# Joined bias loads, spaced weight loads and a later table switch in the prologue; both value blocks of a unit side by side

## The chip, the cores and the metric

The kernel runs on one core of one Trainium2 chip. The metric is device time of one execution in microseconds (us); lower is better. TensorE is called PE, VectorE DVE, ScalarE ACT, GpSimd POOL and SyncE SP, as the profile does.

## The reference, cut to what matters

The input `x` is (128, 32, 512): batch, channel, position. A 32x32 matrix per batch item, picked from 16, mixes the channels; the result goes through an attention over the 32 channels with 32 heads and low-rank queries and keys; then come a masked long convolution over the 512 positions (by FFT in the reference, by Toeplitz matmuls in the kernel) and a dequantised linear layer, with residual sums.

```python
W = weights[condition]                        # (128, 32, 32)
h = einsum('bct,bcd->bdt', x, W)              # tokens are the 32 channels
q_c = h @ Wq_c.T + bq_c                       # 192 wide
q   = (q_c @ Wq_up.T + bq_up)                 # 32 heads of 128 + 64 (rope)
kv  = h @ Wkv_c.T + bkv_c                     # 64 nope + 64 rope
kvu = kv[..., :64] @ Wkv_up.T + bkv_up        # 32 heads: k 128, v 128
k   = concat(k_nope, broadcast(kv_rope))
a   = softmax(q @ k.T / sqrt(192))
o   = a @ v                                   # per head
x   = x + sum_over_heads(o @ Wo.T) + bo
y   = causal_conv(masked x, s4_kernel) + D * masked x     # masked again
x   = x + (y @ dequantised(qweight).T + bias)
```

## The kernel before, in words

The kernel is written with an explicit order for each engine: a function per engine that issues instructions one behind another and waits on semaphores. There is no scheduler; the order on each engine is the order in its function, and a waiting instruction holds all behind it.

The attention is worked off in 16 units (`NU`): 8 groups of 16 batch items (`k`), and of each two halves of 16 heads (unit `u`, group `u // 2`, half `u % 2`). The key up-projection is folded into the query one: for each head a 192x64 matrix M is made once from two weights (`products`, `weights_high`, `weights_low`; 8 weight groups `g` of 4 heads), so the scores are formed against the 64-wide latent. All large matmuls have operands split into a high and a low part, three matmuls for one.

What a unit does, in PE's order (`u` from 2 to 14):
- `fold(u, j0, j1)`: for the heads j0 to j1, latent queries times M into PSUM; two heads at a time in banks 0 and 1 (`BT`) or 2 and 3 (`BS`). Each head is evicted to `qt` by ACT, heads 13 and 15 by DVE (`late_head`). Heads j, j+1 may only start when the two heads four before them are evicted.
- `values(u - 1, m_)`: the probabilities of the unit before times the latent, in two value blocks `m_` of 8 heads, 32 matmuls each (the trace has two records for each, 64 in all), into four PSUM banks. ACT copies each bank to `z_high`, DVE makes `z_low` from bank and copy. Before, `values(u - 1, 0)` stands between heads 0 to 13 and heads 14, 15 of the fold, `values(u - 1, 1)` behind the fold.
- `scores(u, n)`, n = 0 to 3: DVE turns each into `sc` (`take_scores`), takes off the maximum (`below_max`), ACT exponentiates (`soft`), DVE sums, divides and turns (`normalised`) into `pT`.
- `output(u - 1, n)`: z times the value weight, in four parts. In odd units `project` (x times the compressing weights, four token blocks n, per block 8 matmuls with the high and 4 with the low part of x), the copies `feat` of its result on ACT (`feat_taken`) and `mix_features` stand between these parts, for the next group; in even units `turn_latent` follows.

Unit 0 has its own order: `project_first`, `products(0)`, `mix_features(0)`, `products(1)`, then four heads of fold and one `products` in turn, `scores(0, n)`, `products(6)`, `products(7)`. This and unit 1 are called the prologue here. SP issues most transfers in program order, ACT the small bias loads, POOL the gathers of the condition matrices (`gathered`), which it masks into `mix`. The last unit, the convolution and the linear layer (from 575 us on) are not touched.

## Time and profile before

| | us |
|---|---|
| median of 3 runs | 725.34 (724.9 to 725.49) |
| the profiled execution | 725.95 |
| its span in the trace | 724.0 |
| PE busy in the span | 705.0 |
| DVE busy | 597.2 |
| ACT busy | 412.6 |
| POOL busy | 215.3 |

The span is from the first to the last recorded instruction; the profiled execution's own time is 1.95 us longer. A row of the timeline gives start, duration, engine, line and operation, output and inputs, how many instructions stand in the row, and in brackets how long the engine was idle before it and what ended that. Matmuls overlap, so the distance from one start to the next tells more than a duration.

### The profile page before, as it was taken

The numbers are of one execution on the slowest core, as the hardware profiler recorded it, in microseconds if no ns is written. First come the engines' busy times: TensorE is split into PE (matmuls) and PEld (weight loads), VectorE is DVE, ScalarE is ACT, GpSimd is POOL, SyncE is SP. The second block draws the span as 40 slices with busy tenths as digits, with TensorE's granted clock in tenths as the row PEclk, the third lists the DMA queues.
The fourth block names the chain that finished last, engine by engine and source line by source line (L and its number), as shares of the span: only waits on it lengthen the run. The fifth ranks groups of instructions, "written<-read, shape, count | busy, mean of one in ns | idle before, by whom it ended". The sixth has DMA issues, their size and how long they took to land.

```text
span 724.0 us, 17041 instructions
## 1 busy us (share of the span) xinstructions
PE 705.0 (97%) x7154; PEld 567.1 (78%) x7154; DVE 597.2 (82%) x1005; ACT 412.6 (57%) x736; POOL 215.3 (30%) x242
## 2 busy tenths in 40 slices
PE   7999999999999999999999999999999899999997
PEld 6767777787978697878877786978677688888885
DVE  4889999998999678787769776887798689999975
ACT  4676565647556765746565656556664444444443
POOL 5461020020002010550020000003521267777884
PEclk9999999999999999999999999999999999999999
DMA  7900100010002000100100010002112587999942
GB/s 220 329 3 2 51 13 1 2 61 4 1 2 62 3 2 22 39 5 13 60 5 2 2 59 2 1 2 92 60 60 54 139 225 152 181 244 188 239 106 107
DMA packets 31919, 50.94 MB, mean 70 GB/s; under 512 B 6594, under 2 KB 21090, under 8 KB 30562
## 3 DMA queue, kind: packets, MB, share of 16 engines
q1 hardware_dynamic: 29858, 49.26, 25.0%
q8 instruction: 57, 0.93, 0.5%
q0 software_dynamic: 1024, 0.53, 0.4%
q14 instruction: 20, 0.16, 0.1%
q10 hardware_dynamic: 960, 0.06, 0.1%
HBM read 41.19 MB, written 8.63 MB: 69 GB/s over the span
## 4 chain that ended last, share of the span: by engine, by line
PE 76%; DVE 13%; ACT 4%; issue 4%; POOL 2%; DMA 1%; SPq 0%; DVEq 0%; ACTq 0%
PE ps L736 34%; PE ps L785 7%; PE ps L628 5%; PE ps L629 5%; PE ps L630 5%; PE ps L807 4%; PE ps L677 3%; PE ps L636 2%; PE ps L638 2%; PE ps L637 2%; DVE x_low L1663 2%; DVE x_t L1657 2%; DVE y L1701 1%; PE ps L1029 1%; PE ps L1037 1%
## 5 line engine op out<-in xcount | busy, mean ns | idle before, releaser
L1141 ACT ACTIVATE qt<-ps,m_bias 128x512 f32<-128x512 f32 x228 | 145.8, 686 | 87.5 <-PE ps L736 83.9
L736 PE MATMUL ps<-q_high,m_high 64*128 64x512 f32 x768 | 166.0, 397 | 0.2 <-issue 0.2
L736 PE MATMUL ps<-q_high,m_low 64*128 64x512 f32 x768 | 162.4, 388 | 0.2
L736 PE MATMUL ps<-q_low,m_high 64*128 64x512 f32 x768 | 114.4, 387 | 0.0
L736 PEld LDWEIGHTS ps<-q_high,m_high 64*128 64x128 f32 x768 | 89.5, 184 | 15.4 <-issue 5.9
L736 PEld LDWEIGHTS ps<-q_high,m_low 64*128 64x128 f32 x768 | 89.8, 184 | 9.8 <-issue 1.0
L1428 DVE TENSOR_TENSOR z_low<-ps,z_high 128x512 fp32r<-128x512 f32 x128 | 79.8, 681 | 18.7 <-ACT z_high L1161 18.7
L736 PEld LDWEIGHTS ps<-q_low,m_high 64*128 64x128 f32 x768 | 81.6, 184 | 9.8
L1161 ACT CAST z_high<-ps 128x512 fp32r<-128x512 f32 x128 | 66.7, 597 | 14.5 <-PE ps L807 9.9
L1146 ACT ACTIVATE sc<-sc 128x512 f32<-128x512 f32 x60 | 38.1, 634 | 41.5 <-DVE sc L1413 35.2
L494 POOL TENSOR_TENSOR o_sum<-o_part,o_part 128x512 f32<-128x512 f32 x7 | 9.1, 1307 | 173.2 <-ACT o_part L1171 173.2
L459 POOL TENSOR_TENSOR mix<-gathered,block_of 128x256 f32<-128x256 f32 x16 | 10.4, 667 | 161.4 <-PE ps L677 152.1
L785 PE MATMUL ps<-qt,kv 128*32 128x512 f32 x480 | 55.0, 595 | 2.7 <-ACT qt L1141 1.2
L617 POOL TENSOR_TENSOR y_low<-y,y_high 128x512 fp32r<-128x512 f32 x32 | 48.4, 1511 | 18.6 <-ACT y_high L1357 18.5
L628 PE MATMUL ps<-z_high,wvT_high 128*128 128x512 f32 (+1 forms) x132 | 53.6, 406 | 0.0
L1434 DVE TENSOR_SCALAR qt<-ps,m_bias 128x512 f32<-128x512 f32 x28 | 20.9, 750 | 37.7 <-PE ps L736 37.6
L629 PE MATMUL ps<-z_low,wvT_high 128*128 128x512 f32 (+1 forms) x132 | 50.9, 386 | 0.0
L630 PE MATMUL ps<-z_high,wvT_low 128*128 128x512 f32 (+1 forms) x132 | 50.7, 384 | 0.0
L1421 DVE TENSOR_TENSOR sc<-sc,row_stat 128x512 f32<-128x512 f32 x60 | 44.6, 743 | 2.1
L1413 DVE TENSOR_TENSOR sc<-sc,row_stat 128x512 f32<-128x512 f32 x60 | 42.9, 715 | 2.1
L1423 DVE STREAM_TRANSPOSE pT<-sc 128x512 f32<-128x512 f32 x60 | 42.7, 711 | 2.0
L611 POOL TENSOR_TENSOR rest<-rest,x_t 128x512 f32<-128x512 f32 x29 | 37.9, 1308 | 17.0 <-ACT rest L1344 17.0
(259 smaller groups left out, 1468.5 us busy)
## 6 DMA issues: line engine op xcount, KB each, us to landing
x_raw<-in_x_groups SPq DMA_DIRECT2D x32, 256.0 KB
x_t<-in_x_channels SPq DMA_DIRECT2D x8, 1024.0 KB, 7.8
out<-rest SPq DMA_DIRECT2D x32, 256.0 KB, 6.3
toep_high<-taps_scratch SPq DMA_DIRECT2D x32, 192.0 KB, 4.4
toep_low<-taps_scratch SPq DMA_DIRECT2D x32, 192.0 KB, 4.9
w_raw<-in_w_groups SPq DMA_DIRECT2D x8, 512.0 KB, 8.0
toep_far<-taps_scratch SPq DMA_DIRECT2D x32, 64.0 KB, 5.7
rope_raw<-in_rope_rows SPq DMA_DIRECT2D x8, 192.0 KB, 7.7
```

The lines of the kernel that those rows point to most:

```text
L617: pool.tensor_tensor(y_low[g % 2][:, :, ch, :], y[c % 2][:], f(y_high[g % 2][:, :, ch, :]), ALU.subtract).then_inc(s["yl_done"], 1)
L628: pe.matmul(out, lh, rh, start=start, stop=False)
L629: pe.matmul(out, lh, rl, start=False, stop=False)
L630: return pe.matmul(out, ll, rh, start=False, stop=stop)
L736: mm = pe.matmul(ps[:, fold_bank(u, j) + e, :], weights[rows, (GH * g + j) // 2, c, :], moving[c][rows, :], start=start, stop=stop)
L785: mm = pe.matmul(ps[32 * b:32 * b + 32, s_bank(u, n), :], kv[:, tok], qt[:, :, tok], start=True, stop=True)
L1141: act.activation(qt[:, j, :], ps[:, fold_bank(u, j) + j % 2, :], ACT.Identity, bias=m_bias[:, h:h + 1]).then_inc(s["qt_done"], 1)
L1161: act.copy(z_part(z_high, m_, b), z_made(u, m_, b)).then_inc(s["zh_done"], 1)
L1413: dve.tensor_tensor(rows(n), rows(n), wide(n), ALU.subtract).then_inc(s["sub_done"], 1)
L1421: dve.tensor_tensor(rows(n), rows(n), wide(n), ALU.mult).then_inc(s["norm_done"], 1)
L1423: dve.transpose(flat(pT[:, n]), flat(sc[:, n])).then_inc(s["turn_done"], 1)
L1428: dve.tensor_tensor(z_part(z_low, m_, b), z_made(u, m_, b), f(z_part(z_high, m_, b)), ALU.subtract).then_inc(s["zl_done"], 1)
```

## The change

In the prologue:
- The seven small bias loads that ACT issued behind its first casts become three: `bq_bv` (both head biases side by side) is issued by ACT as its second instruction; `latent_biases` (three columns) and `bq_rope` by SP behind weight group 0.
- Weight group 1 is loaded behind the wait for the gathers (it was loaded in front of it), group 2 behind the first mixed block (`q_ready`), groups 3 to 5 each behind a finished `products`, groups 6, 7 and the value weight behind `products(4)`.
- ACT's two sines of the state-space parameters, with the table loads in front of and behind them, move from behind the third `weights_high` inside the fold of unit 0 to behind the last eviction; the four casts of the value weight move into unit 1, and PE's `turned_par` stands four heads later.
- The normalising multiplication of unit 0 moves from DVE to POOL, ahead of POOL's `values_low`; DVE does the four sums and reciprocals first, then the four transposes.

In units 2 to 14:
- The fold of 16 heads is undivided; both value blocks stand behind it, next to each other.
- The second value block of a unit writes banks 0 to 3 (before: 0, 1, 4, 5), and `scores` goes to banks 4, 5, 7, 0 (before: 2, 3, 7, 0). So `scores(u, 0)` waits for the first `z_low` of the first value block, `scores(u, 1)` for the second one; `scores(u, 2)` and `scores(u, 3)` wait for the third and the fifth one, as before.
- `project` does the matmuls with the high part for all four token blocks first, then those with the low part for all four.
- ACT and DVE evict their last heads first and then take the value banks 0 to 3 in one row.

The core of the diff (renamed banks, input packing and the waits that only follow from them are cut):

```diff
@@ sync
-            for g in range(2):
-                load_weights(g)
+            load_weights(0)
+            sp.dma_start(columns[:, 0:3], d["latent_biases"]).then_inc(s["bias_in"], 16)
+            sp.dma_start(m_bias[64:P, :], d["bq_rope"]).then_inc(s["bias_in"], 16)
...
             for n in range(2):
                 sp.wait_ge(gather_in[n], 32)
-            for g in range(2, 6):
+            load_weights(1)
+            sp.wait_ge(s["q_ready"], 1)
+            load_weights(2)
+            for g in range(3, 6):
+                sp.wait_ge(s["fold_ready"], g - 1)
                 load_weights(g)
-            sp.dma_start(wvT_raw[:], d["wvT"]).then_inc(s["wv_in"], 16)
+            sp.wait_ge(s["fold_ready"], 5)
             load_weights(6)
             load_weights(7)
+            sp.dma_start(wvT_raw[:], d["wvT"]).then_inc(s["wv_in"], 16)
@@ tensor, project
-                    if n != 2:
-                        pe.wait_ge(s["s_taken"], 4 * u + (1, 2, 0, 4)[n])
+                    if u == 1 and n < 2:
+                        pe.wait_ge(s["s_taken"], 4 * u + n + 1)
+                    elif n < 3:
+                        pe.wait_ge(s["zl_done"], 8 * (u - 1) + (7, 8, 6)[n])
                     else:
-                        pe.wait_ge(s["zl_done"], 8 * (u - 1) + 6)
+                        pe.wait_ge(s["s_taken"], 4 * u + 4)
...
                         projected(k, n, tt, False)
+                for n in range(4):
                     for tt in range(TT):
@@ tensor, scores
-                if n == 2 and u >= 1:
-                    pe.wait_ge(s["zl_done"], 8 * (u - 1) + 3)
-                if n == 3 and u >= 1:
-                    pe.wait_ge(s["zl_done"], 8 * (u - 1) + 5)
+                if u == 1 and n >= 2:
+                    pe.wait_ge(s["zl_done"], 8 * (u - 1) + 2 * n - 1)
+                if u >= 2:
+                    pe.wait_ge(s["zl_done"], 8 * (u - 1) + (1, 2, 3, 5)[n])
@@ tensor, units 2 to 14
-                    fold(u, 0, 14)
+                    fold(u, 0, 16)
                     values(u - 1, 0)
-                    fold(u, 14, 16)
                     values(u - 1, 1)
@@ scalar, unit 0
-                if g == 2:
-                    act.wait_ge(s["sin_go"], 1)
-                    act.activation(sin1[:], ang[:], ACT.Sin).then_inc(s["sin_done"], 1)
...
-            for n in range(4):
-                values_high(n)
+            act.wait_ge(s["sin_go"], 1)
+            act.activation(sin1[:], ang[:], ACT.Sin).then_inc(s["sin_done"], 1)
...
             weights_high(6)
             weights_high(7)
+            values_high(0)
@@ gpsimd
+            for n in range(4):
+                pool.wait_ge(s["inv_done"], n + 1)
+                pool.tensor_tensor(flat(sc[:, n]).rearrange("p (r c) -> p r c", c=C),
+                                   flat(sc[:, n]).rearrange("p (r c) -> p r c", c=C),
+                                   row_stat[:, n, :].unsqueeze(2).broadcast_to([P, 2 * GP, C]), ALU.mult).then_inc(s["norm_done"], 1)
             for n in range(4):
                 values_low(n)
```

On PE, at the end of unit 2's fold and behind it, before (`q_high` and `q_low` rows are the fold, `pT` rows a value block of 32 matmuls, `qt` the four scores):

```order
L807 MATMUL ps<-pT,ctok 64x128 x32
L736 MATMUL ps<-q_high_71,m_high 128x512 x2
L736 MATMUL ps<-q_high_71,m_low 128x512 x2
L736 MATMUL ps<-q_high_73,m_high 128x512 x2
L736 MATMUL ps<-q_high_73,m_low 128x512 x2
L736 MATMUL ps<-q_high_72,m_high 128x512 x2
L736 MATMUL ps<-q_high_72,m_low 128x512 x2
L736 MATMUL ps<-q_low_74,m_high 128x512 x2
L736 MATMUL ps<-q_low_76,m_high 128x512 x2
L736 MATMUL ps<-q_low_75,m_high 128x512 x2
L807 MATMUL ps<-pT,ctok 64x128 x32
L785 MATMUL ps<-qt,kv 32x512 x16
```

and now:

```order
L753 MATMUL ps<-q_low_74,m_high 128x512 x2
L753 MATMUL ps<-q_low_76,m_high 128x512 x2
L753 MATMUL ps<-q_low_75,m_high 128x512 x2
L824 MATMUL ps<-pT,ctok 64x128 x64
L802 MATMUL ps<-qt,kv 32x512 x16
L641 MATMUL ps<-z_high,wvT_high 128x512
L642 MATMUL ps<-z_low,wvT_high 128x512
```

The last head pair of the fold stands in front of both value blocks, and the scores follow the second block in both orders.

On PE, in `project` of unit 1, before (`x_high` rows are matmuls with the high part of x, eight to a token block, `x_low` rows the four with the low part):

```order
L636 MATMUL ps<-wcT_high,x_low_65 128x320 x2
L636 MATMUL ps<-wcT_high,x_low_66 128x320 x2
L637 MATMUL ps<-wcT_high,x_high 128x320
L638 MATMUL ps<-wcT_low,x_high 128x320
L637 MATMUL ps<-wcT_high,x_high 128x320
L638 MATMUL ps<-wcT_low,x_high 128x320
L637 MATMUL ps<-wcT_high,x_high 128x320
L638 MATMUL ps<-wcT_low,x_high 128x320
L637 MATMUL ps<-wcT_high,x_high 128x320
L638 MATMUL ps<-wcT_low,x_high 128x320
L636 MATMUL ps<-wcT_high,x_low_65 128x320 x2
L636 MATMUL ps<-wcT_high,x_low_66 128x320 x2
```

and now, at the end of the same `project` (`z_high` is the output part behind it):

```order
L651 MATMUL ps<-wcT_low,x_high 128x320
L650 MATMUL ps<-wcT_high,x_high 128x320
L651 MATMUL ps<-wcT_low,x_high 128x320
L649 MATMUL ps<-wcT_high,x_low_65 128x320 x2
L649 MATMUL ps<-wcT_high,x_low_66 128x320 x2
L649 MATMUL ps<-wcT_high,x_low_65 128x320 x2
L649 MATMUL ps<-wcT_high,x_low_66 128x320 x2
L649 MATMUL ps<-wcT_high,x_low_65 128x320 x2
L649 MATMUL ps<-wcT_high,x_low_66 128x320 x2
L649 MATMUL ps<-wcT_high,x_low_65 128x320 x2
L649 MATMUL ps<-wcT_high,x_low_66 128x320 x2
L641 MATMUL ps<-z_high,wvT_high 128x512
```

The low matmuls of all four blocks are now the last 16 of the 48, and the four results become ready close together.

On ACT, in unit 0, before (`qt` rows are evictions of folded heads, `m_high` casts of the folding matrices, `sin` the two sines):

```order
L1141 ACTIVATE qt<-ps,m_bias 128x512 x4
L1112 CAST m_high<-rope_raw 128x6x64
L1115 CAST m_high<-ps 128x6x64
L1212 ACT_TABLE_LOAD
L1212 ACTIVATE sin_125<-ang 32x64
L1213 ACTIVATE sin_126<-ang 32x64
L1214 ACT_TABLE_LOAD
L1214 ACTIVATE warm<-ones 32x1
L1141 ACTIVATE qt<-ps,m_bias 128x512 x4
```

and now:

```order
L1157 ACTIVATE qt<-ps,m_bias 128x512 x4
L1128 CAST m_high<-rope_raw 128x6x64
L1131 CAST m_high<-ps 128x6x64
L1220 ACT_TABLE_LOAD
L1220 ACTIVATE sin_124<-ang 32x64
L1221 ACTIVATE sin_125<-ang 32x64
L1222 ACT_TABLE_LOAD
L1222 ACTIVATE warm<-ones 32x1
L1128 CAST m_high<-rope_raw 128x6x64
L1131 CAST m_high<-ps 128x6x64
L1128 CAST m_high<-rope_raw 128x6x64
```

The last four evictions of unit 0 stand in front of the table loads now, and two pairs of casts of the folding matrices behind them.

## Rows read from the trace of the kernel before

**Rows 1.** The page's first part: busy time of PE.
```profile
PE 705.0 (97%) x7154; PEld 567.1 (78%) x7154; DVE 597.2 (82%) x1005; ACT 412.6 (57%) x736; POOL 215.3 (30%) x242
```
**Rows 2.** Timeline of PE, unit 0: start us, us, engine line op tiles xcount [idle before].
```profile
15.03 0.92 PE L706 MATMUL ps<-w_raw 128*64 128x64 f32 x24 [1.62 <-DMA bq_n<-in_bq_nope]
...
16.06 2.94 PE L677 MATMUL ps<-mix,feat 128*128 128x128 f32 x24
...
24.60 0.92 PE L706 MATMUL ps<-w_raw 128*64 128x64 f32 x24
...
29.94 0.92 PE L706 MATMUL ps<-w_raw 128*64 128x64 f32 x24
...
36.60 0.92 PE L706 MATMUL ps<-w_raw 128*64 128x64 f32 x24
...
44.20 3.64 PE L785 MATMUL ps<-qt,kv 128*32 128x512 f32 x32 [1.16 <-ACT qt L1141]
```
**Rows 3.** Timelines of DVE, POOL and ACT, unit 0.
```profile
14.24 0.21 DVE L1499 COPY feat<-ps 128x64 f32<-128x64 f32 x1
...
9.06 0.95 POOL L449 DMA_INDIRECT gathered<-in_L_cond_weights,row_of  x1 [0.31 <-issue]
...
14.87 0.62 POOL L459 TENSOR_TENSOR mix<-gathered,block_of 128x256 f32<-128x256 f32 x1 [1.42 <-DMA gathered<-in_L_cond_weights,row_of]
...
41.77 2.37 ACT L1141 ACTIVATE qt<-ps,m_bias 128x512 f32<-128x512 f32 x4
```
**Rows 4.** Transfers: w_raw, issue to landing of eight; and qw, on a quiet queue.
```profile
DMA to landing us min/median/max: 7.2/8.0/8.2
...
qw<-in_ffn_words SPq DMA_DIRECT2D x1, 1024.0 KB, 5.2
```
**Rows 5.** Weight loads of PE, waits whose end no record shows, unit 0.
```profile
32.68 0.18 PEld L736 LDWEIGHTS ps<-q_high,m_low 64*128 64x128 f32 x1 [0.53 <-issue]
```
**Rows 6.** Timeline of PE, unit 1: values, scores, project, mixing.
```profile
67.13 1.59 PE L807 MATMUL ps<-pT,ctok 32*64 32x128 f32 x64
...
71.58 1.21 PE L807 MATMUL ps<-pT,ctok 32*64 32x128 f32 x64
...
74.28 1.07 PE L785 MATMUL ps<-qt,kv 128*32 128x512 f32 x8 [0.50 <-DVE z_low L1428]
...
78.13 0.30 PE L637 MATMUL ps<-wcT_high,x_high 128*128 128x320 f32 x1
...
87.69 2.84 PE L677 MATMUL ps<-mix,feat 128*128 128x128 f32 x24
```
**Rows 7.** Timeline of PE, unit 4: the two value blocks and the scores.
```profile
173.25 1.21 PE L807 MATMUL ps<-pT,ctok 32*64 32x128 f32 x64
...
176.66 1.20 PE L807 MATMUL ps<-pT,ctok 32*64 32x128 f32 x64
177.79 3.64 PE L785 MATMUL ps<-qt,kv 128*32 128x512 f32 x32
```
**Rows 8.** Timeline of DVE, unit 4.
```profile
175.11 1.29 DVE L1428 TENSOR_TENSOR z_low<-ps,z_high 128x512 fp32r<-128x512 f32 x2 [0.90 <-ACT z_high L1161]
...
177.46 3.67 DVE L1428 TENSOR_TENSOR z_low<-ps,z_high 128x512 fp32r<-128x512 f32 x6
181.04 2.50 DVE L1407 STREAM_TRANSPOSE sc<-ps 128x512 f32<-128x512 f32 x4
```
**Rows 9.** Timeline of PE, unit 5: project and mixing.
```profile
212.80 0.30 PE L637 MATMUL ps<-wcT_high,x_high 128*128 128x320 f32 x1
...
214.81 0.31 PE L637 MATMUL ps<-wcT_high,x_high 128*128 128x320 f32 x1
...
221.47 2.84 PE L677 MATMUL ps<-mix,feat 128*128 128x128 f32 x24
```
**Rows 10.** Timeline of ACT, unit 5: copies of feat, and an exponential.
```profile
215.01 0.43 ACT L1081 COPY feat<-ps 128x320 f32<-128x320 f32 x1 [2.69 <-PE ps L636]
...
217.19 0.65 ACT L1146 ACTIVATE sc<-sc 128x512 f32<-128x512 f32 x1
```
**Rows 11.** Start of unit 5: ACT's first evictions, and PE's third head pair.
```profile
189.69 1.27 ACT L1141 ACTIVATE qt<-ps,m_bias 128x512 f32<-128x512 f32 x2
...
191.40 0.52 PE L736 MATMUL ps<-q_high,m_high 64*128 64x512 f32 x2
```

More of the change, by code:

```diff
@@ L194, in build @@
     wvT_raw = t("wvT_raw", [P, NPAIR, P], at=wvT_at + 8 * KB)
-    bq_n = t("bq_n", [P, NH], at=zh_at)
-    bv_n = t("bv_n", [P, NH], at=zh_at + 128)
+    bq_bv = t("bq_bv", [P, 2 * NH], at=zh_at)
+    bq_n, bv_n = bq_bv[:, 0:NH], bq_bv[:, NH:2 * NH]
     cond_rows = t("cond_rows", [P, B // 4], I32, at=zh_at + 256)
@@ L293, in build @@
     BT, BS, BZ, BO, BX = 0, 2, 4, 6, 7
-    ZBANK = ((BZ, BZ + 1, BX, BO), (BT, BT + 1, BZ, BZ + 1))
+    FIRST_ZBANK = ((BZ, BZ + 1, BX, BO), (BT, BT + 1, BZ, BZ + 1))
+    ZBANK = ((BZ, BZ + 1, BX, BO), (BT, BT + 1, BS, BS + 1))
     LATE_ZBANK = ((BX, BZ, BZ + 1, BO), (BZ, BZ + 1, BT, BS))
@@ L297, in build @@
     FOLD_BANK = (BT, BS)
-    SBANK = (BS, BS + 1, BX, BT)
+    SECOND_SBANK = (BS, BS + 1, BX, BT)
+    SBANK = (BZ, BZ + 1, BX, BT)
     FIRST_SBANK = (BT, BX, BS, BS + 1)
@@ L919, in _ @@
                     turn_latent(0)
+                    fold(u, 8, 12)
                     turned_par()
-                    fold(u, 8, 16)
+                    fold(u, 12, 16)
                     values(0, 0)
@@ L1209, in _ @@
                 weights_high(g + 2)
[L1210 to L1216 removed]
+            act.wait_ge(s["sin_go"], 1)
+            act.activation(sin1[:], ang[:], ACT.Sin).then_inc(s["sin_done"], 1)
+            act.activation(sin2[:], ang[:], ACT.Sin, scale=0.5).then_inc(s["sin_done"], 1)
+            act.activation(warm[:], ones[:], ACT.Exp)
             weights_high(6)
             weights_high(7)
+            values_high(0)
             for n in range(2):
@@ L1226, in _ @@
             fold(1, 8, 10)
+            values_high(1)
+            fold(1, 10, 12)
+            values_high(2)
             act.wait_ge(s["par_turned"], 1)
             act.copy(parT[:].rearrange("p a h -> p (a h)"), ps[:, BO, 0:4 * C]).then_inc(s["parT_done"], 1)
-            fold(1, 10, 16)
+            fold(1, 12, 14)
+            values_high(3)
+            fold(1, 14, 16)
             for u in range(1, LAST):
@@ L1250, in _ @@
                         ffn_float(2)
-                    values(u - 1, 0, 0, 3)
                     fold(u, 14, 16)
-                    values(u - 1, 0, 3, 4)
+                    values(u - 1, 0, 0, 4)
                     if u == 8:
@@ L1506, in _ @@
             weights_low(1)
+            dve.wait_ge(w_in[0], 32)
+            dve.tensor_reduce(bv_sum[:], bv_n, AX.X, ALU.add).then_inc(s["bias_done"], 1)
             dve.wait_ge(s["ssm_in"], 80)
@@ L1537, in _ @@
             for n in range(4):
-                normalised(0, n)
+                dve.wait_ge(s["exp_done"], n + 1)
+                dve.tensor_reduce(stat(n), rows(n), AX.X, ALU.add).then_inc(s["sum_done"], 1)
+                dve.wait_ge(s["sum_done"], n + 1)
+                dve.reciprocal(stat(n), stat(n)).then_inc(s["inv_done"], 1)
+            for n in range(4):
+                dve.wait_ge(s["norm_done"], n + 1)
+                dve.transpose(flat(pT[:, n]), flat(sc[:, n])).then_inc(s["turn_done"], 1)
             for u in range(1, LAST):
@@ L1557, in _ @@
                 else:
-                    values(u - 1, 0, 0, 2)
                     late_head(u, GH - 1)
-                    values(u - 1, 0, 2, 4)
+                    values(u - 1, 0, 0, 4)
                 values(u - 1, 1, 0, 4)
```

37 lines of the change are left out of this document (14 added, 23 removed).

## The prediction, made before the changed kernel ran

> **What bounds the kernel now.** I read the busy shares first, then PE's timeline by units, then what ended PE's gaps. PE is busy for 705.0 of 724.0 us [rows 1], so time can only come from the 19 us of gaps, from matmuls that are stretched because their operands come late, and from the small loss at each change of kind of matmul. Two stretches matter. In the prologue PE waits visibly: 1.62 us for a bias load, 1.16 us for ACT's evictions [rows 2], and in unit 1 for z_low [rows 6]. In the 13 units from 2 to 14 PE runs almost without a gap: value blocks, head pair and scores follow each other at once [rows 7]. There the change can save only the loss at the changes, and it adds a dependence of the scores on z_low. So I work out both stretches as chains: who is late once the order is new.
>
> **Prologue.** (a) The first mixing starts at 16.06 because products(0) waits for bq_n until 15.03 [rows 2]. With the bias issued at the start, products(0) can begin where project_first ends, 15.03 - 1.62 = 13.41. Next late are DVE's copies of feat, which end at 14.24 + 0.21 = 14.45, and POOL's mix: the last gather is issued until 10.01 and the mask starts at 14.87 [rows 3]. That gather runs beside 704 KB of weight group 1, which now waits. If it lands 1.0 us earlier or more, the copies bound and the mixing starts at 14.55: gain 1.5 us. If it lands as before, the mask ends at 15.49 and the gain is 0.5. I take 1.45, since with group 1 gone less stands beside the gather. The weight loads: group 1 is issued behind the gathers, at about 13.4, and products(1) wants it when the mixing's 2.9 us are over, at 17.4. The eight weight loads landed 7.2 to 8.2 us after issue, in a full queue; twice the size on a quiet queue took 5.2 [rows 4]. I take 4.0, nearer the quiet one less half its bytes: no wait. The bound the other way is 13.4 + 7.2 = 20.6, a wait of 3.2 us. Later groups are asked for at 5.3 us steps and have over 5 us each.
>
> For that load the Trainium skill has a fit: DMA: Bandwidth & Descriptors, "Anatomy of one DMA", gives 2.0 us plus the bytes at 436 KB per us. By it, as an estimate, 512 KB take 3.2 us and products(1) doesn't wait either; the row of 5.2 us for 1024 KB is above its 4.4.
>
> (b) A stretch of one products and four heads takes 29.94 - 24.60 = 5.34 us, the next one 36.60 - 29.94 = 6.66 [rows 2]. The 1.3 us more are waits of PE's weight loads that no record ends, as the one of 0.53 us [rows 5], while transfers fill the engines. If they come from the crowded queue, spaced loads take them away. The last 3.4 MB are still loaded in one go, later. I take 0.9 of 1.3; bounds 0 and 1.6.
>
> The Trainium skill, Runtime: NRT & Kernel Launch, "Instruction fetch mechanics", speaks against (b): it says that a sequential program's fetch is hidden by the issue rate. By it these gaps aren't a matter of the queue and would stay, 0.9 us less gain; no row shows what they wait for.
>
> (c) scores(0, 0) waits 1.16 us for four evictions that began at 41.77, behind two table loads [rows 2, 3]. Without these, the last two evictions end 1.27 us (the duration of such a pair [rows 11]) behind the fold, of which products(5) hides 1.03: 0.24 is left, gain 0.9. The table loads now lie beside scores(0) and products(6), when ACT has only casts to do; POOL's chain on the sines starts some 3 us later and still ends before turned_par.
>
> (d) Unit 1: DVE ends its normalising late, and the scores behind the first value block start late. From 67.13 to the last score block at 74.28 are 7.15 us [rows 6]. The multiplications on POOL free DVE of four of its longest operations; then it is one value block (1.13), two score blocks (1.81), then from the second block's start to the gated score 74.28 - 71.58 = 2.70: 5.64. Gain 1.5. POOL has some 6 us for its four multiplications before the values, and values_low after them before the first output. (e) project of unit 1 to mixing took 9.56 us, waiting for x_low [rows 6]; with the low matmuls last and by (g) it takes 8.93. Gain 0.6. turned_par, apart from turn_latent, costs 0.1. Prologue: -1.45 - 0.9 - 0.9 - 1.5 - 0.6 + 0.1 = -5.3.
>
> **Units 2 to 14.** v is the start of the first value block. (f) Before, v to the scores is 177.79 - 173.25 = 4.54, with a head pair (2.04) inside and two changes of kind, each about 0.1. Undivided, the pair goes before v, and the scores could follow at v + 2.26, a saving of 0.24. But scores(u, 0) now waits for the first z_low. That starts at 175.11 - 173.25 = 1.86 behind v [rows 7, 8], and unit 1 shows the same chain from value block to gated score: 2.70 [rows 6]. ACT is free for it, because its one eviction ends 0.8 behind v. So before: 4.54; after: 2.04 + 2.70 = 4.74. Each unit loses 0.20, 13 units 2.6. The later score blocks find their z_low in time: z_low advances 0.60 a bank (3.67 for six [rows 8]) against 0.91 a score block; the fifth is ready at v + 5.1 for a score at v + 5.4. Bounds: -0.24 and +0.5 a unit.
>
> (g) Odd units 3 to 13: from project to mixing 8.67 us [rows 9], of which 0.25 is a wait for x_low (the first token block takes 2.01, the others 1.76). Without the wait: 8.42. In the new order the four results are ready at 5.3, 5.9, 6.4 and 7.0 behind the start. ACT must copy the first, do an exponential, copy the second, and so on; the last copy ends three exponentials and four copies later. A copy with its small second part takes 0.42 to the next start, an exponential 0.53 (0.65 long, overlapped) [rows 10]: the copies start at 5.47, 6.4, 7.4, 8.3, the last ends at 8.85, and the mixing starts at 8.93. Before, these lay a token block apart under the matmuls. So 8.93 against 8.67: +0.26, six units 1.6. What the low matmuls no longer wait for is more than given back.
>
> (h) Even units: DVE must make eight z_low behind the second block. It starts its turn of the scores at v + 1.86 + 8 x 0.60 = v + 6.64, which is 3.94 behind the scores' start; before it was 181.04 - 177.79 = 3.25 [rows 7, 8]. All that DVE does then, to the exponentials, is 0.69 later against PE, and ACT's first evictions of the next unit stand behind these exponentials. They end at 189.69 + 1.27 = 190.96; PE needs them for the third head pair at 191.40 [rows 11]. With 0.07 for the signal, 0.37 is in hand and 0.69 is asked: a wait of about 0.32, in units 3, 5, 7, 11 and 13 (behind unit 8 the tap products lie before the fold): 1.6. The convolution and the last unit's code are untouched; their wait for DVE may take up to 0.4 of the shift, a bound only.
>
> Sum: -5.3 + 2.6 + 1.6 + 1.6 = +0.5. The profiled execution took 725.95, 0.6 above the median: 726.45, and 725.9 on the median's level.
>
> **The rivals.** First, the forecast, no change. Second, faster: the chains (g) and (h) don't reach PE, because DVE or ACT has slack that I count as used; only (f) is paid. For it: ACT idles 2.69 us before the copies [rows 10]; against it: the copies can't start before their matmuls end. 725.34 - 5.3 + 2.6 = 722.6. Third, faster by more: the undivided fold does what it seems to, scores at v + 2.26: -0.24 x 13 = -3.1 in the place of +2.6, with (g) and (h): 720.1. Against it stands the gated score at 2.70 in unit 1; it would take a z_low that is ready 0.44 sooner than in any row.
>
> Fourth, slower: weight group 1 is late. It lands as the others did, at 20.6 instead of 17.4, products(1) stands in PE's queue before the whole fold, and everything waits 3.2 us: 729.1. For it: every weight load took at least 7.2; against it: they were queued behind one another. It decides from a landing 4.0 us behind its issue on. Fifth, slower: (a) gives only 0.5 and (b) nothing, so the prologue gives 3.4: 727.8.
>
> **How the numbers follow.** A measurement of this kernel tells 0.2%, 1.45 us, from no change. Chances: forecast 0.44, second 0.20, third 0.06, fourth 0.14, fifth 0.16. The forecast's own range is 724.2 to 727.6, since (f) to (h) repeat and 0.1 us a unit is 1.3; some of it lies beyond 726.8. Faster: 0.20 + 0.06 = 0.26. Slower: 0.14 + 0.16 and 0.04 of the forecast = 0.34. Same: 0.40. The range goes to the second case and the fourth: 722.2 to 729.2.
>
> **What the new profile would show.** (a) The first mixing at 14.6, products(1) without a DMA wait. (b) Stretches of 5.3 us between products. (c) No wait over 0.4 us before the first scores. (f) In every unit a gap of PE of 0.4 to 0.5 us before the scores, ended by z_low, and 2.70 from value block to scores. (g) 8.9 us from project to mixing, ended by a copy of feat. (h) A wait of 0.3 us at the third head pair of units 3, 5, 7, 11 and 13, ended by an eviction. The forecast is wrong if the scores follow the value blocks at once, if the mixing doesn't wait for feat, or if products(1) waits for its weights.

## The result

The changed kernel takes 726.18 us (median of 16 runs, 725.35 to 727.74) against 724.76 for the kernel before in the same comparison: ratio 1.0023, 95% interval 1.0014 to 1.0031. That is 1.7 us slower, about at the 0.2% from which a change can be told from none; 725.9 was forecast. One of the 16 runs of before took 865.19 us; the ratio goes by the fast runs alone, and that one isn't among them. The profiled execution took 726.38 us, with a span of 724.5 (before: 725.95 and 724.0).

The end hides two large movements. PE's timeline after, unit 0 and unit 1, answers to [rows 2] and [rows 6] (start us, us, engine, line, operation, tiles, count, [idle before <- what ended it]):

```profile
12.85 0.92 PE L723 MATMUL ps<-w_raw 128*64 128x64 f32 x24
...
14.02 2.94 PE L693 MATMUL ps<-mix,feat 128*128 128x128 f32 x24
16.89 0.92 PE L723 MATMUL ps<-w_raw 128*64 128x64 f32 x24
...
39.67 3.64 PE L802 MATMUL ps<-qt,kv 128*32 128x512 f32 x32 [0.32 <-ACT qt L1157]
...
62.66 1.21 PE L824 MATMUL ps<-pT,ctok 32*64 32x128 f32 x64
...
66.07 1.20 PE L824 MATMUL ps<-pT,ctok 32*64 32x128 f32 x64 [0.35 <-DVE z_low L1439]
...
68.76 1.06 PE L802 MATMUL ps<-qt,kv 128*32 128x512 f32 x8 [0.50 <-DVE z_low L1439]
...
72.63 0.30 PE L650 MATMUL ps<-wcT_high,x_high 128*128 128x320 f32 x1
...
81.57 2.94 PE L693 MATMUL ps<-mix,feat 128*128 128x128 f32 x24 [0.36 <-ACT feat L1098]
```

The lead over the kernel before grows from row to row: the first mixing is at 14.02 in the place of 16.06, the first scores at 39.67 in the place of 44.20, the mixing of unit 1 at 81.57 in the place of 87.69. That is 6.12 us ahead. From there the lead melts, in nearly equal steps but for units 8, 9 and 14. This table gives, from PE's timelines, how far the starts of the scores lie from those of before (negative is ahead):

```
scores of unit         2     3     4     5     6     8    10    12    14   first output projection
changed kernel     -5.81 -5.34 -4.77 -4.30 -3.74 -2.52 -2.05 -0.98 -0.33   +0.46
```

From an even unit to an odd one 0.46 to 0.50 is lost, from an odd one to an even one 0.56 to 0.65. The exceptions are unit 7 to 8 (0.74), unit 8 to 9 (0.18 won back) and unit 13 to 14 (0.19). The view of PE's waits (engine, line, what it waited for: us in total, times, longest) names two large new entries. Below them stand PE's timeline in unit 4 (answers to [rows 7]) and DVE's there (answers to [rows 8]):

```profile
PE ps L802 <- DVE z_low L1439: 7.4, 15, 0.5
PE ps L693 <- ACT feat L1098: 2.5, 7, 0.4
```

```profile
170.32 2.19 PE L824 MATMUL ps<-pT,ctok 32*64 32x128 f32 x128
173.02 3.64 PE L802 MATMUL ps<-qt,kv 128*32 128x512 f32 x32 [0.51 <-DVE z_low L1439]
```

```profile
172.18 4.88 DVE L1439 TENSOR_TENSOR z_low<-ps,z_high 128x512 fp32r<-128x512 f32 x8 [0.97 <-ACT z_high L1177]
176.97 2.50 DVE L1418 STREAM_TRANSPOSE sc<-ps 128x512 f32<-128x512 f32 x4
```

The scores follow the value block by 2.70 us, and DVE begins to turn them 3.95 us behind their start (3.25 before). PE's busy time fell by 3.8 us, and the time didn't: a fall in busy time here only says that its matmuls are stretched less and stand in longer gaps.

```profile
PE 701.2 (97%) x7154; PEld 560.0 (77%) x7154; DVE 590.9 (82%) x1001; ACT 408.5 (56%) x736; POOL 217.6 (30%) x246
```

### The profile page after: what moved, and what is told of

It is laid out like the page before. It is cut to its first block, busy times and chain, and to the rows that moved or that the text cites. A ratio compares the mean times of both kernels' runs of the same rounds, so it can differ in the third digit from the quotient of the medians.

```text
span 724.5 us, 17037 instructions
## 1 busy us (share of the span) xinstructions
PE 701.2 (97%) x7154; PEld 560.0 (77%) x7154; DVE 590.9 (82%) x1001; ACT 408.5 (56%) x736; POOL 217.6 (30%) x246
## 4 chain that ended last, share of the span: by engine, by line
PE 77%; DVE 10%; ACT 7%; issue 4%; POOL 2%; DVEq 0%; ACTq 0%
PE ps L753 37%; PE ps L802 7%; PE ps L641 5%; PE ps L643 5%; PE ps L642 5%; PE ps L693 3%; PE ps L824 3%; PE ps L650 3%; PE ps L651 3%; DVE x_low L1679 2%; DVE x_t L1673 2%; DVE z_low L1439 2%; ACT z_high L1177 2%; ACT sc L1162 2%; DVE y L1717 1%
## 5 line engine op out<-in xcount | busy, mean ns | idle before, releaser
L753 PE MATMUL ps<-q_high,m_high 64*128 64x512 f32 x768 | 158.4, 395 | 0.0
L753 PE MATMUL ps<-q_high,m_low 64*128 64x512 f32 x768 | 155.2, 387 | 0.0
L753 PE MATMUL ps<-q_low,m_high 64*128 64x512 f32 x768 | 110.6, 386 | 0.0
L753 PEld LDWEIGHTS ps<-q_high,m_high 64*128 64x128 f32 x768 | 79.8, 184 | 18.3 <-issue 3.1
L753 PEld LDWEIGHTS ps<-q_high,m_low 64*128 64x128 f32 x768 | 79.9, 184 | 12.1
L753 PEld LDWEIGHTS ps<-q_low,m_high 64*128 64x128 f32 x768 | 76.2, 184 | 12.9
L1177 ACT CAST z_high<-ps 128x512 fp32r<-128x512 f32 x128 | 64.8, 620 | 13.3 <-PE ps L824 8.5
L802 PEld LDWEIGHTS ps<-qt,kv 128*32 128x32 f32 x480 | 16.2, 108 | 35.8 <-issue 33.0
L1424 DVE TENSOR_TENSOR sc<-sc,row_stat 128x512 f32<-128x512 f32 x60 | 41.7, 696 | 2.1
L1432 DVE TENSOR_TENSOR sc<-sc,row_stat 128x512 f32<-128x512 f32 x56 | 40.6, 724 | 1.9
```

Of the source, the lines that this page charges most:

```text
L753: mm = pe.matmul(ps[:, fold_bank(u, j) + e, :], weights[rows, (GH * g + j) // 2, c, :], moving[c][rows, :], start=start, stop=stop)
L802: mm = pe.matmul(ps[32 * b:32 * b + 32, s_bank(u, n), :], kv[:, tok], qt[:, :, tok], start=True, stop=True)
L1177: act.copy(z_part(z_high, m_, b), z_made(u, m_, b)).then_inc(s["zh_done"], 1)
L1424: dve.tensor_tensor(rows(n), rows(n), wide(n), ALU.subtract).then_inc(s["sub_done"], 1)
L1432: dve.tensor_tensor(rows(n), rows(n), wide(n), ALU.mult).then_inc(s["norm_done"], 1)
```

## The experiments

Twelve runs were made, of ten kernels (pj_again and p_again repeat pj_copies and p_only), in three groups; the kernels of a group shared a chip and its runs of before. Below the first two rows the groups are the first four, the next four and the last four. "To mixing" is the time from the projection's start to the mixing in unit 3, the next two are between the starts of the scores of units 2, 3 and 4; "gaps" is what products(1) to products(5) of unit 0 took above 21.36 us.

```
kernel          ratio    95% interval     to mixing  2 to 3  3 to 4   gaps
before          1                             8.67    28.59   38.31   1.65
changed         1.0023   1.0014-1.0031        8.94    29.06   38.88   0.00
p_only          0.9955   0.9939-0.9971        8.68    28.59   38.31   0.01
old_project     1.0056   1.0041-1.0071        9.38    29.03   39.21   0.02
h_fix           1.0005   0.9995-1.0014        8.95    28.73   38.87   0.00
copies_first    0.9981   0.9972-0.9991        8.42    29.02   38.25   0.02
units_only      1.0089   1.0075-1.0103        8.95    29.04   38.89   1.54
pj_copies       0.9933   0.9920-0.9946        8.43    28.60   38.05   2.07
unspaced        1.0043   1.0028-1.0059        8.95    29.03   38.93   2.24
biases_only     0.9987   0.9977-0.9996        8.69    28.59   38.32   4.30
hg_fix          0.9963   0.9950-0.9977        8.42    28.73   38.30   0.00
norm_on_dve     1.0032   1.0020-1.0044        8.95    29.02   38.87   0.00
pj_again        0.9928   0.9914-0.9941        8.42    28.56   38.05   0.01
p_again         0.9950   0.9937-0.9964        8.68    28.59   38.31   0.00
```

### 1. The two halves apart: p_only and units_only

p_only is the changed kernel with these lines (and the orders of work that belong to them) as before; units_only is the reverse, those lines on the old prologue.

```diff
-    ZBANK = ((BZ, BZ + 1, BX, BO), (BT, BT + 1, BS, BS + 1))
+    ZBANK = ((BZ, BZ + 1, BX, BO), (BT, BT + 1, BZ, BZ + 1))
-    SBANK = (BZ, BZ + 1, BX, BT)
+    SBANK = (BS, BS + 1, BX, BT)
...
-                    fold(u, 0, 16)
+                    fold(u, 0, 14)
                     values(u - 1, 0)
+                    fold(u, 14, 16)
                     values(u - 1, 1)
```

> The prologue's edits alone (joined biases, spaced weight loads, later tables, POOL's multiplications, spread casts of the value weights), with the divided fold, the old banks and the old order of the projection in every later unit. Theory (the sum as predicted: the prologue gives, units 2 to 14 take back): the trace of the changed kernel stood 5.8 us ahead at unit 2, and nothing in the old units takes it back, so 719.5 us, 0.9920 of before, range 718.5 to 721. Rival A (the lead is lost somewhere behind the prologue whatever the units look like, in the convolution or the last unit): 723 to 725, over 0.997. In the trace: 8.67 us from project to mixing and 4.54 us from value block to scores, as before.

Measured 0.9955. The trace bears the theory out: 5.04 us ahead at unit 2, between 5.04 and 5.36 in every unit to the last, 5.1 at the end. The lead isn't lost elsewhere. But the timed runs give only 3.3 us (a span of 718.9 against 724.0 would be 5.1): the median of 720.55 lies in the range of 718.5 to 721, and the forecast ratio of 0.9920 lies outside the interval. Its second measurement says the same (0.9950, 3.6 us). The one profile of before has 1.65 us of gaps in unit 0, and the difference is of that size; what the timed runs of before have there no record shows.

> The undivided fold, its banks and the new order of the projection on the prologue of before. Theory (prologue and units add up): the unit costs that the traces have shown (0.48 us from even to odd and 0.57 us from odd to even, 13 steps, less 0.6 in the first projection) make 5 to 6 us more than before: ratio 1.0068 by the two measured ratios (1.0023 of the changed kernel over 0.9955 of the prologue alone), range 1.005 to 1.009. Rival (the units' cost exists only because the shorter prologue leaves some engine behind): 1.002 or less.

Measured 1.0089, at the top of the range. The steps are those of the changed kernel (29.04 and 38.89), so they don't come from the shorter prologue; the rival falls. The two ratios make 1.0044 together where the changed kernel has 1.0023; that is within the three intervals taken together.

### 2. Step (g): old_project and copies_first

```diff
@@ old_project, on the changed kernel
                         projected(k, n, tt, False)
-                for n in range(4):
                     for tt in range(TT):
@@ copies_first, on the changed kernel
-                    for n in range(3):
-                        feat_taken(i // 2, n)
-                        soft(u, n)
-                    feat_taken(i // 2, 3)
+                    for n in range(4):
+                        feat_taken(i // 2, n)
+                    for n in range(3):
+                        soft(u, n)
```

> The changed kernel with the old order inside the projection (the low matmuls of a token block right behind its high ones), all else as changed. Theory (step g): the mixing comes 8.67 us behind the start of the projection in the place of 8.94, and the seven odd units with their 0.36 us waits for a copy of feat give back 1.6 to 2 us against the changed kernel: ratio to before near 0.9997 where the changed kernel has 1.0023. Rival (the wait is bought by a later start of what follows on DVE, so that the difference is taken back in the next even unit): the same time as the changed kernel within 0.5 us, 1.002.

Both wrong: it is slower than the changed kernel, 1.0056. The mixing doesn't come after 8.67 but after 9.38. Timelines of PE and DVE of this kernel, the projection of unit 5:

```profile
209.79 0.30 PE L650 MATMUL ps<-wcT_high,x_high 128*128 128x320 f32 x1
...
211.64 0.41 PE L649 MATMUL ps<-wcT_high,x_low 128*128 128x320 f32 x1 [0.19 <-DVE x_low L1384]
```

```profile
207.32 2.50 DVE L1417 STREAM_TRANSPOSE sc<-ps 128x512 f32<-128x512 f32 x4
209.74 2.45 DVE L1384 TENSOR_TENSOR x_low<-x_raw,x_high 128x512 fp32r<-128x512 f32 x4
```

and DVE of the kernel before in the same place, with the projection at 212.80 [rows 9]:

```profile
209.63 2.50 DVE L1407 STREAM_TRANSPOSE sc<-ps 128x512 f32<-128x512 f32 x4
212.06 2.45 DVE L1374 TENSOR_TENSOR x_low<-x_raw,x_high 128x512 fp32r<-128x512 f32 x4
```

x_low begins 0.05 ahead of the projection here and 0.74 before. The 0.69 by which the undivided fold makes DVE late, which I had followed to the fourth exponential of even units only, stands ahead of x_low in odd units and makes the old order 0.71 slower (8.67 to 9.38). The new order takes 0.44 of that back. So the new order of the projection isn't a cost of 0.26 but a mending of 0.44 for a cost of 0.71 that belongs to the fold.

> The changed kernel, but ACT does the four copies of feat in a row and then the three exponentials, in the odd units. Theory (step g: the order of ACT's work between the copies is what holds the mixing): the last copy ends 0.4 us behind the last matmul of the projection, the output between hides it, and the mixing comes 8.4 to 8.5 us behind the start of the projection in the place of 8.94: seven times 0.45, some 3 us less than the changed kernel, ratio to before near 0.998. Rival (the exponentials, up to 1.7 us later, make the cast of the next latents on ACT or DVE's normalising late, and the head pairs or value block of the next unit wait): 0 to 2 us slower than that, ratio 1.001 or more.

Right: 0.9981 and 8.42 from project to mixing, with ACT's copies of feat no longer apart. It brings 3.0 us against the changed kernel. The two weren't measured beside each other; by the ratios it is 0.0042 of the time, and in the profiles this kernel loses 1.99 us against before from unit 2's scores to unit 14's, where the changed kernel loses 5.48.

### 3. Step (h): h_fix

```diff
+                    else:
+                        soft(u - 1, 3)
...
-                    for n in range(4):
+                    for n in range(3 if u < LAST - 1 else 4):
                         soft(u, n)
```

(The first part stands behind `fold(u, 0, 2)` in the odd units' loop.)

> The changed kernel, but behind an even unit ACT evicts the first two heads of the next unit ahead of the fourth exponential (it does so already behind an odd unit). Theory (step h): the third head pair of units 3, 5, 7, 11 and 13 starts without its 0.3 us wait, 1.6 us less than the changed kernel, ratio to before near 1.0001. Rival 1 (the third head pair isn't late because of the exponential): nothing, 1.002. Rival 2 (the fourth exponential, some 1.3 us later, makes DVE's normalising and with it the next value block late): slower than the changed kernel by over 1 us.

Right: 1.0005, 1.3 us by the ratios. ACT in the changed kernel, and in this one, behind unit 4 (one fence each):

```profile
184.77 0.63 ACT L1162 ACTIVATE sc<-sc 128x512 f32<-128x512 f32 x1 [0.69 <-DVE sc L1424]
185.31 0.35 ACT L1123 COPY ctok<-ps 128x256 f32<-128x256 f32 x1
185.56 2.62 ACT L1157 ACTIVATE qt<-ps,m_bias 128x512 f32<-128x512 f32 x4
```

```profile
184.10 0.35 ACT L1123 COPY ctok<-ps 128x256 f32<-128x256 f32 x1
185.00 1.27 ACT L1157 ACTIVATE qt<-ps,m_bias 128x512 f32<-128x512 f32 x2 [0.55 <-PE ps L753]
186.16 0.63 ACT L1162 ACTIVATE sc<-sc 128x512 f32<-128x512 f32 x1
```

ACT now waits for PE and not PE for ACT, and the third head pair follows the second by 2.04 us (184.67, 186.71) in the place of 2.34 (184.54, 186.88 in the changed kernel):

```profile
184.67 0.52 PE L753 MATMUL ps<-q_high,m_high 64*128 64x512 f32 x2
...
186.71 0.52 PE L753 MATMUL ps<-q_high,m_high 64*128 64x512 f32 x2
```

The step from even to odd fell from 29.06 to 28.73; 0.14 stays above before's 28.59. The two ratios weren't measured beside each other either, and their intervals touch; the step of 0.33 us in the traces is the firmer sign.

### 4. Step (f) alone: hg_fix, and the divided fold beside it: pj_copies, pj_again, p_again

hg_fix has the edits of h_fix and of copies_first. pj_copies (pj_again is the same) is p_only with the new order of the projection and the copies first:

```diff
                         projected(k, n, tt, False)
+                for n in range(4):
                     for tt in range(TT):
...
+                    for n in range(4):
+                        feat_taken(i // 2, n)
...
```

> The changed kernel with both mendings on ACT: the fourth exponential of even units behind the next unit's first two evictions, and the four copies of feat ahead of the three exponentials. Theory (of the three unit costs only step f is left): from project to mixing 8.42, even units to odd ones 28.7 to 28.8 between starts of the scores, odd to even 38.2 to 38.3 (before: 28.59 and 38.31); value block to scores 2.70 everywhere with its gap of 0.5 us. By the ratios so far 1.0023 - 0.0018 - 0.0042 = 0.9963, range 0.995 to 0.9975; against the divided fold with the same order (pj_again) it is 0.2 us a unit slower, 2.6 us. Rival (the undivided fold costs nothing by itself, the gap of 0.5 us only stands where the changes of kind stood before): as fast as pj_again, 0.993 to 0.994.

Right: 0.9963, and on the same chip 720.97 against 718.42 of pj_again: 2.55 us, where 13 times 0.20 is 2.6. In the profiles the scores of unit 14 lie 2.45 us further behind those of unit 2 than in pj_again, but not in 12 equal steps: most differ by 0.13 to 0.25, unit 5 to 6 by 0.66, unit 7 to 8 by 0.38, unit 8 to 9 by 0.04, and unit 13 to 14 by -0.18. That the sum comes so near to 2.6 is in part luck. The wait for the first z_low is the part of the undivided fold's cost that neither of the two edits of ACT's order takes away.

> The new prologue, the divided fold and the old banks, the new order of the projection, and on ACT the four copies of feat ahead of the three exponentials. Theory: from project to mixing 8.42 us in the place of 8.67 in six units and about 8.5 in the place of 9.54 in the first: 2 to 2.6 us less than the prologue alone, ratio 0.9923, and 4.54 from value block to scores everywhere. It would be the fastest of all. Rival (the exponentials behind the copies make DVE's normalising and the next value block late, which the undivided fold's slack hid): 0.995 or more.

Right within its interval: 0.9933. Each odd-to-even step is 0.17 to 0.26 shorter than before: 38.05 in the place of 38.31 from unit 3 to 4.

> The same kernel as pj_copies, beside the prologue alone and the mended undivided fold on one chip. Its first profile had 2.07 us of gaps between the products of unit 0 that the other executions with spaced loads had not. Theory (such gaps are chance with spaced loads, and the rule only with the crowded queue): stretches of 5.34 this time, profiled time near the median, ratio 0.993. Rival (they belong to this kernel's order): 2 us again.

Right: no gap this time, 718.42 us, ratio 0.9928. It is the fastest kernel tried: by the ratios 5.2 us below before and 6.9 below the changed one (0.9928 against 1.0023).

> The same kernel as p_only, on the chip of pj_again. Theory: the new order of the projection with the copies first is worth 1.1 us in unit 1 and 0.25 us in six units on the divided fold, so this is 2.6 us slower than pj_again, ratio 0.9965 against 0.993; first profile: 0.9955 and no gaps in unit 0. Rival (that order gives only what the traces showed in units 2 to 14): 1.5 us slower.

The rival is right: 720.00 against 718.42, 1.6 us. In the profiles unit 1's mixing is 1.30 us earlier in pj_again than in p_again (1.13 by the order, 0.17 from a projection that began earlier), and half is given back at once, because PE waits for q_low, the low part of the next latents. PE of pj_again, then DVE of pj_again and of p_again (one fence each):

```profile
87.98 0.50 PE L748 MATMUL ps<-q_low,m_high 64*128 64x512 f32 x2 [0.39 <-DVE q_low L1401]
```

```profile
83.06 2.44 DVE L1461 SCALAR_TENSOR_TENSOR o_sum<-o_sum 128x512 f32<-128x512 f32 x3
85.53 0.75 DVE L1388 SCALAR_TENSOR_TENSOR q_low<-ps,columns,q_high 128x512 fp32r<-128x512 f32 x1
```

```profile
83.23 2.14 DVE L1460 SCALAR_TENSOR_TENSOR o_sum<-o_sum 128x512 f32<-128x512 f32 x3
85.40 0.75 DVE L1387 SCALAR_TENSOR_TENSOR q_low<-ps,columns,q_high 128x512 fp32r<-128x512 f32 x1
```

ACT's casts aren't what is late: they follow the mixing by the same 1.09 us in both. DVE has no pause ahead of q_low. It works through its operations on o_sum (angles for the convolution) and comes to q_low at the same time in both kernels, however early the mixing is. So DVE's own order is the next thing that holds this place. At unit 2's scores 0.63 of the 1.30 is left. The odd-to-even steps after that add 0.14 to 0.26 each, with no such wait.

### 5. Steps (a) and (b): biases_only and unspaced

```diff
@@ biases_only, on the kernel before (ACT's part is cut)
-            for g in range(2):
-                load_weights(g)
+            load_weights(0)
+            sp.dma_start(columns[:, 0:3], d["latent_biases"]).then_inc(s["bias_in"], 16)
+            sp.dma_start(m_bias[64:P, :], d["bq_rope"]).then_inc(s["bias_in"], 16)
+            load_weights(1)
...
@@ unspaced, on the changed kernel
-            load_weights(1)
-            sp.wait_ge(s["q_ready"], 1)
-            load_weights(2)
-            for g in range(3, 6):
-                sp.wait_ge(s["fold_ready"], g - 1)
-                load_weights(g)
-            sp.wait_ge(s["fold_ready"], 5)
-            load_weights(6)
-            load_weights(7)
+            for g in range(1, 8):
+                load_weights(g)
```

> The kernel before with the joined biases alone: bq and bv as one load at the start of ACT's queue, the latents' biases as one and the rope's bias behind weight group 0 on SP's queue. Group 1 stays at once behind them, beside the gathers, and the other groups behind the gathers, unspaced. Theory 1 (step a, the bias load was what held the first mixing, and the copies of feat are next): the mixing starts at 14.0 to 14.6 in the place of 16.06, about 1.7 us gained, ratio 0.9975. Theory 2 (the last gather is held by group 1's 704 KB beside it and is next): the mixing starts near 15.5, gain 0.5, and the later time of group 1 is needed for the rest. In both: the gaps of 1.3 us and more in unit 0 and the wait of 1.16 us ahead of the first scores stay.

Between the theories: the mixing starts at 14.72 and it is POOL's mix that ends its wait.

```profile
12.43 0.92 PE L708 MATMUL ps<-w_raw 128*64 128x64 f32 x24
13.18 0.35 PE L714 MATMUL ps<-bq_bv,w_raw 128*64 128x1 f32 x8
14.72 0.46 PE L679 MATMUL ps<-mix,feat 128*128 128x128 f32 x2 [1.19 <-POOL mix L461]
```

```profile
8.65 0.94 POOL L451 DMA_INDIRECT gathered<-in_L_cond_weights,row_of  x1 [0.30 <-issue]
...
13.96 0.61 POOL L461 TENSOR_TENSOR mix<-gathered,block_of 128x256 f32<-128x256 f32 x1 [1.27 <-DMA gathered<-in_L_cond_weights,row_of]
```

The last gather is used 13.96 - 9.59 = 4.37 us behind the end of its issue. In the changed kernel, where group 1 waits, it is 13.04 - 9.85 = 3.19; before it was 4.86 [rows 3]. Over all profiles it is 3.19 to 3.99 where group 1 waits (eleven of them, median 3.65) and 4.37, 4.86 and 4.92 where it doesn't. So group 1 beside the gather costs about 1.2 us between the medians. In this profile its delay would have paid, since the mask was what the mixing waited for. But 14.72 lies within the 14.02 to 14.99 of the kernels that delay group 1, so what the delay adds at the mixing isn't clear of chance. The ratio, 0.9987, is 0.9 us.

> The changed kernel with the weight groups 1 to 7 issued in one go behind the gathers, and the weights of the values behind them (no wait between the groups). Theory (step b, the crowded queue stretches the issue of PE's weight loads): the stretches between two products in unit 0, now 5.34 us each, grow again to 5.6 to 6.7, in all 1.0 to 1.65 us, ratio to before near 1.004. Rival (the gaps went because of something else, the tables or the order of code, or because they aren't the queue's): the stretches stay 5.34 us and the ratio 1.002.

Right: the stretches between products are 6.31, 5.34, 6.61 and 5.34 in the place of 5.34 each, and 2.24 us are lost there. The ratio, 1.0043, is 1.5 us above the changed kernel's, with intervals that touch. PE's timeline shows a wait that no record ends:

```profile
31.11 0.28 PE L722 MATMUL ps<-bq_bv,w_raw 128*64 128x1 f32 x3 [1.06 <-issue]
```

All four profiles with unspaced loads have such gaps (1.5 to 4.3 us), and nine of ten with spaced ones have none. The tenth, pj_copies, had 2.07, and its profiled time (722.84) stood 2.2 above its median; its repetition had none. Crowded transfers make the gaps likely, but they aren't needed for them. What PE waits for is open.

### 6. Step (d): norm_on_dve

```diff
-            for n in range(4):
-                pool.wait_ge(s["inv_done"], n + 1)
-                pool.tensor_tensor(...)
...
             for n in range(4):
-                dve.wait_ge(s["exp_done"], n + 1)
...
+                normalised(0, n)
```

> The changed kernel with the four multiplications of unit 0 back on DVE (sum, reciprocal, multiplication, turning for each block in turn), all else as changed. Theory (step d, DVE's normalising held the first value block and the first scores of unit 1): from the start of unit 1's value block to its last score block 7.1 us again in the place of 6.1, and the value block itself may start later; about 1 us more than the changed kernel, ratio 1.0037. Rival (POOL's detour gives nothing, because the second value block and the fourth exponential hold the same place): within 0.3 us of the changed kernel, 1.002.

The theory falls, by the trace; the ratio of 1.0032 isn't clear of the changed kernel's 1.0023. From the first value block to the gated score are 69.35 - 63.25 = 6.10 us, the same as with POOL's multiplications, where the kernel before has 7.15.

```profile
63.25 1.21 PE L819 MATMUL ps<-pT,ctok 32*64 32x128 f32 x64
64.67 1.92 PE L797 MATMUL ps<-qt,kv 128*32 128x512 f32 x16 [0.21 <-issue]
...
69.35 1.07 PE L797 MATMUL ps<-qt,kv 128*32 128x512 f32 x8 [0.50 <-DVE z_low L1434]
```

The 0.4 us at its end stands already in the prologue ahead of it (its first mixing is at 14.61). What set unit 1 free is seen on DVE of the kernel before, beside POOL:

```profile
51.77 1.22 DVE L1413 TENSOR_TENSOR sc<-sc,row_stat 128x512 f32<-128x512 f32 x1
52.92 1.65 DVE L1396 TENSOR_TENSOR m_low<-rope_raw,m_high 128x384 fp32r<-128x384 f32 x1
54.58 0.56 DVE L1399 TENSOR_TENSOR m_low<-ps,m_high 128x384 fp32r<-128x384 f32 x1
...
56.02 1.50 DVE L1413 TENSOR_TENSOR sc<-sc,row_stat 128x512 f32<-128x512 f32 x1
```

```profile
51.16 5.81 POOL L513 TENSOR_TENSOR wvT_low<-wvT_raw,wvT_high 128x512 fp32r<-128x512 f32 x4 [0.19 <-POOL par L551]
```

The subtraction takes 0.69 elsewhere and the first kind of m_low 0.59. While POOL's four subtractions of the value weights ran, they took 1.22, 1.65 and 1.50, which costs DVE 2.4 us in all. In the changed kernel ACT's casts of the value weights are spread, and POOL's subtractions come behind. The same operations take 0.69, 0.59 and 0.84 there, in the order of the rows. Only operations with both inputs in SBUF are stretched; m_low with an input in PSUM keeps 0.56. The Trainium skill, SBUF — State Buffer, "SBUF: two separate sides", says that a DVE operation with two SBUF inputs and a GpSimd operation that reads SBUF lock each other out; these rows agree: 1.22 to 1.65 us beside POOL, 0.59 to 0.69 without it, and 0.56 with an input in PSUM.

norm_on_dve allows a check, since DVE has the same work in it and no pause either. From the first scores to the end of its normalising DVE takes 23.98 us before (68.18 - 44.20) and 22.87 in norm_on_dve (63.13 - 40.26), 1.11 less. There one multiplication is stretched, again beside a subtraction of POOL, and three other operations by 0.07 to 0.17:

```profile
60.74 1.65 DVE L1427 TENSOR_TENSOR sc<-sc,row_stat 128x512 f32<-128x512 f32 x1
```

```profile
60.55 1.29 POOL L521 TENSOR_TENSOR wvT_low<-wvT_raw,wvT_high 128x512 fp32r<-128x512 f32 x1 [0.29 <-ACT wvT_high L1131]
```

In all that is 1.3 us of stretching in the place of 2.4, and the difference is the 1.1. So the stretching accounts for the gain; that the spread casts alone moved POOL's subtractions was read from these rows and not run by itself.

## Why the prediction was right, step by step

The sum was right (+0.5; the profiles say +0.4, the timed runs +1.4 to 1.7), partly by luck. Errors in it had both signs: the prologue gave more in the profiles than forecast, and the units took more. The 725.9 lies so near the 726.18 because the forecast stood on a median of 725.34 for before, which took 724.76 in the comparison; as a difference the forecast is about a third of what the timed runs show.

- (a) predicted -1.45, came -2.04. The gather did land earlier, as taken, and group 1 was no wait, so the slower rival fell. The mixing was held by DVE's copies. Nearly all of the 0.59 us more is a projection that ended 0.56 earlier, mostly because the last x tile came earlier (ACT cast it at 9.46, before at 9.88). The weight groups landed in 4.3 us (median), where 4.0 was taken. The fit of the Trainium skill that the prediction set beside it (DMA: Bandwidth & Descriptors, "Anatomy of one DMA") stands there for transfers that GpSimd issues; these are SP's, and its 3.2 us was too short. Across the eleven profiles with this start of the prologue the first mixing lies between 14.02 and 14.99, so this part is chance, and 14.55 lies in its middle.
- (b) predicted -0.9, came -1.65 in the profiles: the upper bound. Unspaced loads bring the gaps back (2.24). From the rule of the Trainium skill weighed against this step (Runtime: NRT & Kernel Launch, "Instruction fetch mechanics") the prediction read that they would stay; they went. The rule speaks of instruction fetches alone, so this doesn't go against it: no run shows what the gaps wait for.
- (c) predicted -0.9, came -0.84: products(5) to scores are 39.67 - 38.25 = 1.42 in the place of 2.26. No wait over 0.4.
- (d) predicted -1.5, came -1.05. The size is 0.45 off, since the second value block waits 0.35 for z_low, which my chain left out; and the cause was wrong. I put it on DVE's multiplications; taking them back to DVE changes nothing, and the rows point to POOL's subtractions beside DVE.
- (e) predicted -0.6, came -0.62.
- (f) predicted 2.70 from value block to scores and 0.20 a unit: 2.70 came in every unit but the ninth (2.80), and 0.20 was lost in eleven of the thirteen. In units 9 and 14 the kernel before had a wait of 0.3 to 0.4 of its own (4.98 and 4.92 from value block to scores), so there 0.14 and 0.18 were gained: 1.9 us in all and not 2.6. hg_fix against pj_again gave 2.55. The third case, scores at v + 2.26, is refuted.
- (g) predicted 8.93 to the mixing and +0.26: 8.94, ended by a copy of feat, and the order of ACT's work is what holds it (8.42 with the copies first). The attribution failed: against the old order under the same fold the new order gains 0.44. I had left out that (h)'s 0.69 is ahead of x_low as well.
- (h) predicted 0.32 in five units: 0.30 at the third head pair, and h_fix takes it away.
- Left out: 0.10 us in each odd-to-even step between mixing and value block (20.81 against 18.67 + 2.04), five times, and 0.26 ahead of unit 8. In old_project, copies_first and hg_fix the 0.10 is gone, but 0.17 to 0.18 stays ahead of unit 8, and copies_first and hg_fix have 0.4 ahead of unit 6, where PE's q_low matmuls are stretched. Between unit 14's scores and the last unit's another 0.5 goes, 0.29 of it a wait of unit 14's last score block:

```profile
517.99 1.07 PE L802 MATMUL ps<-qt,kv 128*32 128x512 f32 x8 [0.29 <-DVE z_low L1439]
```

With the last unit (+0.3, inside its bound of 0.4) the way from unit 1's mixing to the first output projection costs 6.6 and not 5.8.

Prologue -6.1 and units +6.6 make the profiles' +0.46. The two sizes are off by 0.8 each, and they cancel. In the timed runs the prologue gives about 3.5, which is the size of the fifth case, though not for its reasons: the profile shows all of (a) and (b). The profile of before was one execution; how often its 1.65 us of gaps occur stays open.

## What to carry to other kernels

Where the engine that bounds the time runs without gaps, moving its own work to save changes of kind only pays if the work that is moved away covered no chain of other engines. Here the head pair covered a chain of PE, ACT, DVE and back of 2.70 us, and every later consumer on DVE inherited 0.69 us. Follow such a delay to all that stands behind it on the delayed engine, not only to the first that is late. When a chain through a second engine sets a start, put that engine's gating operations ahead of its patient ones (feat copies ahead of exponentials gave 3 us of 726), and then look what has become the next wait (here DVE's q_low behind o_sum).

## What was not expected of the hardware

- DVE operations with both inputs in SBUF took 1.22 to 1.65 us in the place of 0.59 to 0.69 while POOL ran tensor operations of 1.3 to 1.5 us; those with an input in PSUM and reductions (0.67) weren't stretched.
- The last indirect gather was used 3.2 to 4.0 us behind the end of its issue with SP's second weight group held back (eleven profiles), and 4.4 to 4.9 beside these 704 KB (three). A weight group of 512 KB landed in 4.3 us (median of eight) when spaced and in 8.0 in the crowd.
- PE's unexplained gaps of 1.5 to 4.3 us in unit 0 come and go from execution to execution, with every crowded queue and with one in ten of the spaced ones. One profile of a prologue isn't its typical time: profiled executions with gaps stood up to 2.3 us above their medians (and that of copies_first 2.9, with none).
